# Another hand-written order of the steps in a transformer-layer kernel

## The reference

```python
x = x + layernorm(attention(layernorm(x)))   # 16 query heads, 8 key heads, D = 128, causal
x = x + layernorm(ffn(layernorm(x)))         # width 1024
# attention, per pair of query heads (0 and 1 of the pair, each with its own keys):
p = softmax(q0 @ k0.T * scale) - lam * softmax(q1 @ k1.T * scale)
o = p @ v                                    # v is 256 wide
o = o * rsqrt(mean(o * o) + 1e-5) * subln_w * (1 - LAMBDA_INIT)
out = o @ out_w.T + out_b
# ffn: Walsh-Hadamard transform, up and gate projection, silu(gate) * up,
# Walsh-Hadamard transform, down projection
```

## Time and profile before

| | us |
|---|---|
| median of 3 runs | 1372.66 |
| lowest and highest | 1372.49, 1372.67 |
| the profiled execution, its time | 1372.67 |
| its span | 1370.9 |
| PE busy | 1349.5 (98%) |
| VectorE busy | 1025.5 (75%) |
| ScalarE busy | 889.8 (65%) |
| GpSimd busy | 868.7 (63%) |

### The profile page before, as it was taken

How to read it: one execution, slowest core, us unless ns; L and a number is a source line. 1 busy time by engine, 2 the same in 40 slices (tenths; PEclk the granted TensorE clock), 3 DMA queues, 4 the chain that set the end, 5 groups by cost and what they waited for, 6 DMA issues and landing times.

```text
span 1370.9 us, 26493 instructions
## 1 busy us (share of the span) xinstructions
PE 1349.5 (98%) x8328; PEld 1204.2 (88%) x8328; DVE 1025.5 (75%) x2585; ACT 889.8 (65%) x2499; POOL 868.7 (63%) x1353
## 2 busy tenths in 40 slices
PE   8999999999999999999999999999999999999998
PEld 7888999889988999889889999889799888887787
DVE  7877877876777777866877777866778888856545
ACT  6666676765676766765676666666667877765442
POOL 2765766655666666655676656646767778776443
PEclk9999999999999999999999999999999999999999
DMA  4000000000000000000000000000100100000001
GB/s 136 1 32 1 1 2 1 16 2 1 32 1 2 1 1 1 17 1 1 31 1 1 1 1 1 20 1 1 48 1 1 32 16 1 17 31 1 27 17 35
DMA packets 10072, 18.50 MB, mean 13 GB/s; under 512 B 976, under 2 KB 7888, under 8 KB 9424
## 3 DMA queue, kind: packets, MB, share of 16 engines
q1 hardware_dynamic: 8304, 15.10, 3.3%
q10 hardware_dynamic: 1632, 1.70, 0.4%
HBM read 14.71 MB, written 2.10 MB: 12 GB/s over the span
## 4 chain that ended last, share of the span: by engine, by line
PE 86%; DVE 5%; POOL 4%; ACT 2%; issue 2%; DMA 0%; ACTq 0%; POOLq 0%; DVEq 0%
PE score_bank L732 8%; PE score_bank L734 8%; PE score_bank L733 8%; PE turn_bank L757 7%; PE score_bank L853 6%; PE proj_bank L757 5%; PE sum_bank L757 4%; PE turn_bank L759 4%; PE turn_bank L741 4%; PE turn_bank L804 4%; PE turn_bank L818 3%; PE proj_bank L759 3%; PE sum_bank L741 2%; PE sum_bank L759 2%; PE proj_bank L741 2%
## 5 line engine op out<-in xcount | busy, mean ns | idle before, releaser
L888 ACT ACTIVATE e<-score_bank,negmx 128x512 f32<-128x512 f32 (+3 forms) x640 | 395.0, 626 | 101.8 <-DVE negmx L1114 100.9
L1362 POOL TENSOR_TENSOR e<-e,e 128x384 f32<-128x384 f32 (+3 forms) x256 | 296.9, 1160 | 21.4
L1110 DVE TENSOR_REDUCE mx<-score_bank 128x1 f32<-128x512 f32 (+1 forms) x384 | 242.1, 638 | 36.5 <-PE score_bank L734 35.4
L732 PE MATMUL score_bank<-k_hi,q_hi 128*128 128x512 f32 (+3 forms) x640 | 257.8, 403 | 5.1 <-ACT e L888 3.6
L1345 POOL TENSOR_TENSOR inv_s<-s,neg_one 128x1 f32<-128x1 f32 x128 | 71.1, 556 | 275.5 <-DVE s L1329 275.3
L734 PE MATMUL score_bank<-k_hi,q_lo 128*128 128x512 f32 (+3 forms) x640 | 231.6, 362 | 0.0
L733 PE MATMUL score_bank<-k_lo,q_hi 128*128 128x512 f32 (+3 forms) x640 | 231.2, 361 | 0.0
L1359 POOL TENSOR_SCALAR e<-e,ratio 128x384 f32<-128x384 f32 (+3 forms) x256 | 179.0, 699 | 12.2
L1105 DVE CUSTOM_DVE_ANT_0 score_bank<-score_bank,mask 128x384 f32<-128x384 f32 (+3 forms) x256 | 143.4, 560 | 50.4 <-PE score_bank L734 49.0
L757 PE MATMUL turn_bank<-v_hl,pT_hi 128*128 128x512 f32 x484 | 176.8, 399 | 1.0 <-DVE pT_lo L1120 0.8
L732 PEld LDWEIGHTS score_bank<-k_hi,q_hi 128*128 128x128 f32 x640 | 120.7, 189 | 20.5 <-ACT e L888 5.9
(11 more groups left out here) (382 smaller groups left out, 3591.9 us busy)
## 6 DMA issues: line engine op xcount, KB each, us to landing
w_raw<-in_w_qkv_dram SPq DMA_DIRECT2D x3, 1024.0 KB, 4.8
w_raw<-in_w_o_dram SPq DMA_DIRECT2D x4, 512.0 KB, 3.4
w_raw<-in_w_ug_dram SPq DMA_DIRECT2D x4, 512.0 KB, 4.2
bv<-in_hidden_dram SPq DMA_DIRECT2D x8, 256.0 KB, 3.0
out_dram<-e SPq DMA_DIRECT2D x16, 128.0 KB, 1.7
e<-in_w_d_dram SPq DMA_DIRECT2D x1, 1024.0 KB, 4.7
x_in<-in_hidden_dram ACTq DMA_DIRECT2D x3, 256.0 KB, 4.8
x_in<-in_hidden_dram SPq DMA_DIRECT2D x3, 256.0 KB, 4.4
```

Source lines behind the costliest of these rows:

```text
L732: pe.matmul(bank[:, 0:w], qh, kh, start=True, stop=False)
L888: act.activation(e, S[k % NS][:, 0:w], ACT.Exp, bias=negmx[:, d % 2, m, s:s + 1], accum_out=ssum[:, d % 4, s, m, c:c + 1]).then_inc(s_act, 1)
L1110: dve.tensor_reduce(mx[:, d % 2, m, s, c:c + 1], S[k % NS][:, 0:w], X, ALU.max)\
L1362: pool.tensor_tensor(a, a, b, ALU.add).then_inc(p_pool, 1)
```

## The change

It rewrites the order and nothing else: the strings of `HALVES`, `HEAD`, `TURN_OF_GROUP`, `LAST_GROUP` and `LAST_HALVES`, the list `FIRST_STEPS` and the table `WITH_GATED`. The number of steps of each kind stays, with 36 idle transposes in the place of 34. Two exceptions go from the tables of lags: step `X` 5 on ACT and `QP (1,0,0)` on DVE. One condition on ACT is written in another way. Which work bank a step gets, and the step to which an exponential or a mix is attached, follow from the order and so change too.

```diff
--- before.py
+++ after.py
@@ -59,47 +59,46 @@
 
 
 
-HALVES = ('TSTTSSTSPoSQTOTPPP', 'STSTSOTSTTPSoQPPP')
+HALVES = ('STSTSSTTPSToTQPPPO', 'STSTSSOTPTSoQPPPT')
 HEAD = {
-    3: 'QTSTSSPSSP', 4: 'TSSTSSTPTAoPSQTPTPO', 5: 'TSTASSATOSQAPSoPTPPKT', 6: 'STSTSSTQSPPoTTPPTO',
-    7: 'STSSTKOSSToPQPTPTP', 8: 'TTSSSSTTToPSQPPPTVO', 9: 'STSTSOSTVPSoQTVPPTP', 10: 'STTSSSTPTSoQTPPPTO'}
+    3: 'TSQTSSPSSP', 4: 'TSSTSSTPTASoQTPPTPO', 5: 'TSTASSATOASQPSoPPTPT', 6: 'TSKSTSSTPQSoTTPPPTO',
+    7: 'STSSTKOSTSoPQPTPPT', 8: 'TSTSSSTToPTSQPPPTVO', 9: 'TSTSSOSTVPSVoQTPPTP', 10: 'STTSSSTPTSoQTPPPTO'}
 FIRST_HALF = 3
 TURN_OF_GROUP = {
-    0: 'STSKTPKoTSPTSSTKPTQOPK', 2: 'TTSSTVSVSQVSVoTPPTTVPPVOV', 3: 'TSSVTSOTPSTSoTQPPP',
-    27: 'STSTSkTSPOTSoQwPPTP', 28: 'STTTSSSTPoSQPOTTPP', 31: 'STKTTSKSPKSTOToSKPQPP'}
+    0: 'TSSTSKPTTKSSoQPKTTPPOK', 2: 'TSSTTVSPSQSoTPPPTTOVVV', 3: 'VTSSVTSOVTVSPSTQToPPP',
+    27: 'TSTSSTkSOPTSoQwPPPT', 28: 'TSTSSTSoPTPSQOTPPT', 31: 'TSKTSKSPSTKOSoQTPKTPP'}
 
 
 LAST_GROUP = {
-    5: 'STTSTOSSPSoTQPTPHP', 12: 'TSSTSSTToSPbQTPPTOP', 13: 'bTSSSOSTNPSTTNoQPPTP', 14: 'STSTSSTPSTNoQNPPTPTO',
-    15: 'SNTSTSNOSoPTSfNQPPTTP', 16: 'TSSTSSPoSTfTTQPNfPTPO', 17: 'TSTSOSTPSNSoQNTPPTbP',
-    18: 'TSSTSSTPTNSfPTPNoPTOQ', 19: 'STTSfSOSTPoQPTSPPT', 20: 'STTSSSTPTSobTQPPPTO',
-    21: 'TSTSSNPOSfToSNQTPTfPP', 22: 'TSSTSSTPNTSoQTPPTPO', 23: 'TSSTSNOSTPfSoNTQPPPT',
-    24: 'TSSTSSTPNbTSoQPPNNTbTPO', 25: 'TTSSNOSPSToSQNPTTPP', 26: 'TSSTTSSPoNTSfQPTTPNPO',
-    27: 'TSTSSTOPSSfoQTPPTP', 28: 'TSfTSTSSPbSTfoTPQPbTOP', 30: 'TSSTSSfTPTSfoPQPfTPTO',
-    31: 'STTSSOoPfTTSSPPPQT'}
+    5: 'TSTTSOSSPSoTQPTPHP', 12: 'TTSSSSTPbTSoQPTPbPTO', 13: 'TSSOSTSNPSTNoTQPPTP', 14: 'TSSTSSTPNTSoQNPPTPTO',
+    15: 'TSTSSNOSoPTSfNQTPPTP', 16: 'TSSTSSPSNoTTfTQPNfPPTO', 17: 'TSTSOSSNTPSoQNTPPTbP',
+    18: 'TSSTSSTPNTSfPTPNPoTOQ', 19: 'bSTTSSOSTPoQPTSPPT', 20: 'TTSSSSTPTSfoQTPPPTO',
+    21: 'TSTSSNPOSfToSNQTPPTfP', 22: 'TSSTSSTPNTSoQTPNPPTO', 23: 'TSSTSNOSTPfSoQTPPTP',
+    24: 'TSSTSSTPNbTSoQTPPNNbTPO', 25: 'TSTSNOSSPToSQNTTPPP', 26: 'TSSTTSSPoNTSfQTPTPNPO',
+    27: 'TSTSSOTPSSfoQTPPTP', 28: 'TSSfTSSTPbTSfoTPQPbTOP', 30: 'TTSSSSfTPTSfoQPPfTPTO',
+    31: 'TSTSSOTPSSfoQTPPTP'}
 
 
 FIRST_STEPS = (
-    ("LN", 0), ("LN", 1), ("NX", 0), ("IDLE", 34), ("WK", 0), ("X", 0), ("X", 1), ("IDLE", 6), ("NX", 1),
+    ("LN", 0), ("LN", 1), ("NX", 0), ("WK", 0), ("IDLE", 36), ("X", 0), ("X", 1), ("IDLE", 6), ("NX", 1),
     ("LN", 2), ("K", (0, 0, 0)), ("X", 2), ("K", (0, 1, 0)), ("X", 3), ("WQ", 0), ("K", (0, 0, 1)), ("NX", 2),
     ("K", (0, 1, 1)), ("X", 4), ("X", 5), ("QP", (0, 1, 0)), ("QP", (0, 1, 1)), ("S", (0, 0, 0)), ("WV", 0),
-    ("S", (0, 0, 1)), ("LN", 3), ("QP", (0, 0, 0)), ("K", (0, 0, 2)), ("K", (0, 1, 2)), ("S", (0, 0, 2)),
-    ("S", (0, 0, 3)), ("NX", 3), ("S", (0, 0, 4)), ("QP", (0, 0, 1)), ("S", (0, 1, 0)), ("V", (0, 0)),
-    ("S", (0, 1, 1)), ("V", (0, 1)), ("S", (0, 1, 2)), ("V", (0, 2)), ("LAM", None), ("S", (0, 1, 3)),
+    ("S", (0, 0, 1)), ("LN", 3), ("K", (0, 0, 2)), ("QP", (0, 0, 0)), ("K", (0, 1, 2)), ("S", (0, 0, 2)),
+    ("QP", (0, 0, 1)), ("S", (0, 0, 3)), ("NX", 3), ("S", (0, 0, 4)), ("LAM", None), ("S", (0, 1, 0)),
+    ("V", (0, 0)), ("S", (0, 1, 1)), ("V", (0, 1)), ("S", (0, 1, 2)), ("V", (0, 2)), ("S", (0, 1, 3)),
     ("V", (0, 3)), ("S", (0, 1, 4)), ("S", (1, 0, 0)), ("QP", (1, 0, 0)), ("V", (0, 4)), ("S", (1, 0, 1)),
-    ("QP", (1, 1, 0)), ("QP", (1, 0, 1)), ("S", (1, 0, 2)), ("S", (1, 0, 3)), ("S", (1, 0, 4)))
+    ("QP", (1, 0, 1)), ("S", (1, 0, 2)), ("QP", (1, 1, 0)), ("S", (1, 0, 3)), ("S", (1, 0, 4)))
 
 WITH_GATED = {
-    1: (("N", (2, 0, 0)), ("N", (2, 0, 1)), ("DB", 0), ("DB", 1), ("DB", 2)), 2: (("DB", 3), ("N", (2, 1, 0))),
-    4: (("N", (2, 1, 1)), ("DB", 4)), 5: (("DB", 5), ("NA", (2, 0)), ("NA", (2, 1)), ("DB", 6)),
-    6: (("DB", 7), ("DB", 8), ("DB", 9)), 7: (("N", (2, 2, 0)), ("N", (2, 2, 1))),
-    9: (("DB", 10), ("DB", 11), ("DB", 12), ("DB", 13), ("DB", 14)),
-    11: (("DB", 15), ("N", (2, 3, 0)), ("N", (2, 3, 1)), ("FH", 8)), 12: (("FH", 9),),
-    13: (("F", 8), ("F", 9)), 14: (("FH", 10), ("FH", 11)),
-    15: (("F", 10), ("F", 11), ("Z", (2, 0)), ("Z", (2, 1)), ("N", (3, 0, 0)), ("N", (3, 0, 1)), ("N", (3, 1, 0)), ("N", (3, 1, 1)), ("NA", (3, 0))),
-    17: (("NA", (3, 1)),), 20: (("N", (3, 2, 0)),), 21: (("N", (3, 2, 1)),),
-    23: (("N", (3, 3, 0)), ("N", (3, 3, 1)))}
-LAST_HALVES = ('TUTUTToUUoUUOPP', 'OTTUOTPPTP', 'UTTTToUUPOUoPoPU')
+    1: (("N", (2, 0, 0)), ("N", (2, 0, 1)), ("DB", 0), ("DB", 1), ("DB", 2)), 3: (("DB", 3),),
+    5: (("N", (2, 1, 0)), ("N", (2, 1, 1)), ("DB", 4), ("DB", 5)),
+    6: (("NA", (2, 0)), ("NA", (2, 1)), ("DB", 6), ("DB", 7), ("DB", 8)), 7: (("DB", 9), ("N", (2, 2, 0))),
+    9: (("N", (2, 2, 1)), ("DB", 10), ("DB", 11), ("DB", 12), ("DB", 13)), 10: (("DB", 14),),
+    11: (("DB", 15), ("N", (2, 3, 0)), ("N", (2, 3, 1))), 12: (("FH", 8), ("FH", 9)), 13: (("F", 8), ("F", 9)),
+    14: (("FH", 10), ("FH", 11)), 15: (("F", 10), ("F", 11), ("Z", (2, 0)), ("Z", (2, 1))),
+    17: (("N", (3, 0, 0)), ("N", (3, 0, 1))), 18: (("N", (3, 1, 0)), ("N", (3, 1, 1)), ("NA", (3, 0))),
+    19: (("NA", (3, 1)),), 20: (("N", (3, 2, 0)),), 22: (("N", (3, 2, 1)), ("N", (3, 3, 0)), ("N", (3, 3, 1)))}
+LAST_HALVES = ('TUTUoUTPToPUO', 'UTUUTTUTPOPPO', 'UToTTTUUPOoPoPU')
 
 DVE_MIXES = (3,)
 
@@ -117,10 +116,10 @@
 
 SCALAR_LAGS = {
     "K": 1, "V": 1, "QP": 0, "OP": 0, ("K", (0, 0, 0)): 0, ("K", (0, 1, 1)): 0, ("V", (0, 0)): 2,
-    ("V", (0, 3)): 2, ("V", (0, 4)): 2, ("X", 5): 1}
+    ("V", (0, 3)): 2, ("V", (0, 4)): 2}
 VECTOR_LAGS = {
     "WK": 1, "PV": 1, "T": 1, "OT": 1, "Z": 1, "F": 1, "WO": 1, "K": 1, "V": 1, "X": 1, "FH": 1, "U": 1,
-    ("QP", (1, 0, 0)): 1, ("V", (0, 1)): 0, ("V", (0, 4)): 0, ("X", 3): 0}
+    ("V", (0, 1)): 0, ("V", (0, 4)): 0, ("X", 3): 0}
 
 
 FFN_CHUNKS = SEQ // BANK
@@ -934,7 +933,7 @@
                     elif kind == "K":
                         g, m, c = what
                         act.wait_ge(kv_full, kv_use[kind, what] + 1)
-                        if kv_use[kind, what] == 0:
+                        if g == 0 and m == 0 and c == 0:
                             act.wait_ge(cols_landed, 16)
                         at = K_COL + 2 * g + m
                         act.activation(k_hi[:, m, c * BANK:(c + 1) * BANK], bank_for(kind, what)[:, :],
```

## The result

| us | before | after |
|---|---|---|
| median of 4 runs | 1372.66 | 1382.09 |
| lowest and highest | 1372.49, 1372.79 | 1381.48, 1382.47 |
| profiled execution, its span | 1372.67, 1370.9 | 1380.84, 1379.0 |

The ratio is 1.0068 with an interval of 1.0051 to 1.0086: slower by more than 0.2%, outside the range of 1369.0 to 1380.0. The profiled execution ran at a granted clock of 1.000 and is 1.3 us faster than the median; the other four show 0.998 or 0.999.

A forecast was written before the change was run, and what follows sets the result against it. TensorE (PE) was taken as the bound; 2.1 + 1.4 + 0.9 + 0.4 + 0.4 − 1.1 − 1.8 − 0.7 = +1.6 us on 1372.67 gave 1374.3 us, with a range of 1369.0 to 1380.0.

The forecast's parts named there:

- transposes to products: Products wait for pT_lo where fewer steps separate them from their transposes; 0.5 each at (18,3) and (34,3); +2.1 us.
- first scores, duos 19 and 35: Scores wait for bank-freeing exponentials: 0.9 at 11 first scores, 0.5 for halves of duos 19 and 35; +1.4 us.
- S (14,0,1) and repeats: Score at 271.07 and two repeats, already waiting for an exponential, come 0.33 sooner: 0.3 each, +0.9 us.
- small reuses, last group: Thirteen work banks retaken within 2.0 us, +0.4; last group's redistributed norm and fold steps put DVE work behind other scores, +0.4.
- waits removed in the middle: Two waits for e shrink, −0.4, and late scores of duo 14 and repeats go, −0.7; −1.1 us.
- OP 96: OP step at 970 us gets a bank freed earlier, so its wait behind o_sum goes: −1.8 us.
- head, up to 120 us: Moved LAM gives DVE and ScalarE back some of the head's 3.0 us of waits for e: −0.7 us.
- mixes: DVE's mix one step behind transposes with close products at 14 places costs nothing if short: 0.
- (d): Rival: the 14 DVE mixes grow from 0.80 half-way to 1.83 us: +5.6, 1379.9 us; chance 0.06.
- (a): Rival: acc on DVE ahead of the next half's scores delays pT_lo at 12 tight chunks: 5.0 more, 1379.3; chance 0.16.
- (c): Rival: the wait at 970 us only moves to the transposes behind it: +1.8, 1376.1 us; chance 0.10.
- (b): Rival: ScalarE and DVE run ahead, so only the removed waits count: −3.6, 1369.1 us, faster; chance 0.18.

The follow-up runs named there:

- later mixes: VectorE's mixes placed one step later on VectorE alone: on the changed kernel 1374.40 us, on the kernel before 1368.10 us.
- the string of half 21: Changed kernel with the last group's half 21 string as before (TfPP for PPTfP at its end), which moves the mix of chunk (58,3): 1379.53 us.
- the third part alone: Kernel before with only LAST_GROUP, WITH_GATED and LAST_HALVES changed (also called the last part alone): 1375.19 us, ratio 1.0018.
- that one line: Kernel before with VectorE's mixes later on VectorE alone: one step 1368.10 us, two steps 1365.84 us.
- the parts of the rewritten order that helped: Kernel before with mixes two steps later, plus the change's FIRST_STEPS, lags, WITH_GATED and a new string in the last group's half 4: 1364.27 us.
- The kernel with halves 22 and 23 undone: Changed kernel with the last group's strings of halves 22 and 23 as before: 1380.59 us, ratio 1.0058.

## Why the prediction was wrong

By its own steps, in us of the profiled executions:

| step | forecast | measured | |
|---|---|---|---|
| transposes to products | +2.1 | +1.3 | mechanism and the largest two right to 0.02 |
| first scores, duos 19 and 35 | +1.4 | under +0.4 | the scores do start 0.14 to 0.19 behind their exponentials, as (12,0,0) and (13,0,0), but lose 0.05 or nothing by it: the 0.07 of spare was laid out too short |
| S (14,0,1) and repeats | +0.9 | +1.5 | |
| small reuses, last group | +0.4, +0.4 | +3.6 (2.6 at QP steps), +3.8 in the last group (2.0 at S (59,0,4)) | **the step that failed** |
| waits removed in the middle | −1.1 | −1.4 | |
| OP 96 | −1.8 | −1.9 | |
| head, up to 120 us | −0.7 | +0.6 | S (1,0,4) −1.0 and OT 1 −0.5 as hoped, OP 0 +1.4 not seen |
| mixes | 0 | (in the row of the small reuses) | |

The failed step is "small reuses", together with the sentence that the mix "costs nothing as long as it is short". I looked at how long VectorE's mix lasts and at how far each product stands from its transposes. I did not ask how long VectorE stands in front of the mix. The rows had it: the same answer that gave the mix's durations also says that VectorE stood idle before it for 6.3 us in 11 places. With a `pT_lo` or a mask behind the mix, such a standing of 1.1 to 1.5 us delays it, and PE meets it as a bank that is not free. The later mixes show this for the six QP steps, 2.6 us, and together with the string of half 21 for S (59,0,4), 2.0 us: these waits go, and those at PV (18,3) and (34,3) and at S (14,0,1) stay. At two of the six, QP (10,1,1) and (18,1,1), it was the other half of the sentence that failed: the mix was not short, 1.74 us.

This is where the terms were mis-sized, 4.6 of the 7.4 us measured in that row. It is only a small part of why the new order as a whole is slower. The kernel before paid for its own mixes, which I hadn't seen either, and with later mixes on both the changed kernel is still 6.8 us longer by the spans. What then remains against my +1.6 us is in places that I had at 0.04 each or hadn't looked at: thirty waits of about 0.1 us in the middle (2.9), OP 0 (1.4), and F 0, T (50,1), T (55,1) and S (60,1,4) (0.6 to 0.7 each). The runs show these places and that they don't hang on the mixes; what makes the small ones stays open.

The second fault is the ceiling. I read 1.75 us of idle in the middle as the most that could be gained there. In starts the kernel before had about 5 us of waits in that stretch, of which later mixes removed 3.5.

Of the rivals, (d) came nearest in size (1379.9) and (a) next (1379.3). (a) is right in that VectorE's queue is late; its cause, `acc` in front of the scores, is not what the rows show. (d) is wrong as stated: the mixes did not grow and have a median of 0.81 us, as before. What it says of a long mix holds at QP (10,1,1) and (18,1,1) alone.

```profile
L1336 DVE SCALAR_TENSOR_TENSOR e<-e,ratio,e x64: 609/812/1745, 45.4 to 1222.9; 128x384 f32<-128x384 f32 x32, 128x512 f32<-128x512 f32 x32
...
  POOL ratio L1349: 8.8, 12
```

(c) is partly right: T (50,1) waits 1.0 instead of 0.35. (b), faster, is refuted. What stays open is about 1 us between the sum of the parts and the whole, the small waits in the middle, the cause of F 0 and T (55,1), which the third part alone reproduces but no smaller change was tried on, and how the pair of `wo_lo` divides between VectorE's own work and GpSimd. On that, the Trainium skill, page "SBUF — State Buffer", section "SBUF: two separate sides", has the rule that a VectorE operation with two SBUF inputs and a GpSimd operation that reads SBUF shut each other out. The pair takes 0.88 us at 968 us, where GpSimd runs only short operations on one column or nothing, and 1.67 to 1.98 beside GpSimd's mixes in the head, which agrees with it; no run here took GpSimd's work away.

## What to carry to other kernels

In an in-order queue, ask of each instruction that waits for another engine what stands behind it, not only how long it runs: a wait that harms nobody becomes PE's wait when one mask moves behind it. Then test the suspect on the kernel before as well as on the changed one: here it costs both, and most of the difference between them lies elsewhere. Before reordering by hand the steps that everyone shares, try the same step later on one engine only; here that one line gave −4.9 and then −7.0 us on the kernel before, and the parts of the rewritten order that helped gave 1.6 more. And where PE is 99.8% busy by the profile, count its instructions in a stretch: waits shorter than the overlap of two matmuls show as busy time.

## What was unexpected in the hardware's numbers

A product starts 0.05 to 0.07 us behind the end of its `pT_lo` at some places, (8,3) and (9,3) of the changed kernel, and 0.13 to 0.15 at others, (10,2) and (18,3). Whether it had to wait does not decide which: (61,4) waited 0.7 us and stands at 0.05, (10,2) waited for nothing and stands at 0.13. What does decide it stays open.

Small differences of the granted clock go with small differences of time in some kernels and not in others. The kernel with halves 22 and 23 undone took 1380.41 to 1380.86 us in four runs at 1.000 and 1381.99 in one at 0.998. The kernel with the last part alone took 1374.44 to 1375.35 in six runs at 1.000 and 1375.19 to 1376.60 in four at 0.998. The kernel before, run beside them, took 1372.44 to 1373.46 in ten runs at 1.000 and 1372.66 to 1373.53 in five at 0.998, which is the same. Where the two go together, the difference, about 1 us, is as large as the effects of single strings.
